# A product of constants in every slot of the quantised attention, and four query heads of batch two turned by transposes on TensorE

## What is computed

```
q = (x @ Wq + bq).reshape(1, B * N, H, hd)          # 256 queries, 16 heads of 16
kv = (cond @ Wkv + bkv).reshape(1, -1, 2, H, hd)    # 4096 keys and values
q, k, v = q * scale (hd ** -0.5), kv[:, :, 0], kv[:, :, 1]
q = _fq_sym(q, axis=-1)       # rounded to 127 steps of each row's largest
k = _fq_sym(k, axis=-1)
v = _fq_sym(v, axis=2)
attn = softmax(einsum('bhqd,bhkd->bhqk', q, k))
attn = _fq_unsigned(attn, axis=-1)                  # 255 steps of each row's largest
out = einsum('bhqk,bhkd->bhqd', attn, v) @ Wp + bp
```

## Time and profile before

| | us |
|---|---|
| median of the runs (3) | 698.59 |
| lowest and highest run | 698.45, 702.17 |
| profiled execution, its own time | 700.33 |
| its span, first to last instruction | 699.0 |
| PE busy in the span | 659.5 (94%) |
| DVE busy | 573.9 (82%) |
| ACT busy | 413.6 (59%) |
| POOL busy | 389.1 (56%) |
| mean granted TensorE clock | 0.873 |

### The profile page before, as it was taken

The page is one execution under the profiler, slowest core; times in us unless marked ns, Lnnn a source line. Parts: engine busy times, 40 slices in busy tenths (PEclk is TensorE's granted clock), DMA queues, the critical chain, the costliest instruction groups (busy, mean ns, idle before and its releaser), DMA issues. The chain is left out here.

```text
span 699.0 us, 13832 instructions
## 1 busy us (share of the span) xinstructions
PE 659.5 (94%) x5080; PEld 400.2 (57%) x5080; DVE 573.9 (82%) x1029; ACT 413.6 (59%) x689; POOL 389.1 (56%) x500
## 2 busy tenths in 40 slices
PE   9899999999999999999999999888899699989996
PEld 7456766666666767767676667634354234333462
DVE  5998978887897797899898687987888697999555
ACT  5744454445444555647546345378889597799831
POOL 5878557585576636789963444555546333345401
PEclk9999999999999999999999999976568555555589
DMA  9565899656658599989867876679999699799900
GB/s 309 150 151 129 166 188 182 136 138 143 143 129 157 130 197 230 160 203 178 192 140 164 167 168 147 140 138 225 216 175 177 114 198 177 128 180 168 168 1 8
DMA packets 351219, 112.06 MB, mean 160 GB/s; under 512 B 317096, under 2 KB 347824, under 8 KB 351152
## 3 DMA queue, kind: packets, MB, share of 16 engines
q1 hardware_dynamic: 351152, 111.17, 78.1%
HBM read 31.97 MB, written 0.26 MB: 46 GB/s over the span
## 5 line engine op out<-in xcount | busy, mean ns | idle before, releaser
L1061 PE MATMUL psum<-c_nat,eT 128*128 128x256 f16 x1536 | 187.9, 273 | 1.5 <-ACT u_sb L1235 1.2
L1895 DVE TENSOR_REDUCE tops<-psum 128x1 f32<-128x512 f32 x256 | 160.2, 681 | 23.0 <-PE psum L1846 22.2
L1888 ACT ACTIVATE cT<-psum,bias,q_scale 128x1024 f16<-128x1024 f32 x128 | 153.2, 1202 | 27.1 <-PE psum L1846 25.6
L1033 PE MATMUL psum<-cT,qk 128*128 128x512 f16 x744 | 165.6, 379 | 0.1
L1061 PEld LDWEIGHTS psum<-c_nat,eT 128*128 128x128 f16 x1536 | 147.2, 98 | 24.5 <-issue 2.3
L1846 PE MATMUL psum<-kT,v_space 32*128 32x512 f16 x512 | 111.6, 556 | 14.3 <-DVE tops L1895 5.9
L1033 PEld LDWEIGHTS psum<-cT,qk 128*128 128x128 f16 x744 | 72.6, 98 | 82.3 <-issue 1.2
L1273 DVE TENSOR_REDUCE neg_max<-psum 128x1 f32<-128x2048 f32 x32 | 73.2, 2287 | 24.2 <-PE psum L1033 23.9
L1261 DVE TENSOR_TENSOR e_lo<-e_all,e_hi 128x2048 f16<-128x2048 f32 x32 | 87.8, 2744 | 0.0
L1204 ACT ACTIVATE e_all<-psum,neg_max 128x2048 f32<-128x2048 f32 x32 | 63.1, 1970 | 15.4 <-DVE neg_max L1275 15.4
L1846 PEld LDWEIGHTS psum<-kT,v_space 32*128 32x128 f16 x512 | 24.0, 97 | 77.6 <-DVE tops L1895 31.7
(11 more groups left out here) (283 smaller groups left out, 984.4 us busy)
## 6 DMA issues: line engine op xcount, KB each, us to landing
wvo_h<-in_L_xattn_Wv SPq DMA_DIRECT2D x30, 128.0 KB, 2.5
wvo_h<-in_L_xattn_Wo SPq DMA_DIRECT2D x30, 128.0 KB, 2.3
wqk_h<-in_L_xattn_Wq SPq DMA_DIRECT2D x28, 128.0 KB, 2.4
wqk_h<-in_wkT SPq DMA_DIRECT2D x28, 128.0 KB, 2.7
mx_land<-in_mx_weights SPq DMA_DIRECT2D x8, 384.0 KB, 4.1
v_space<-in_ctx SPq DMA_DIRECT2D x4, 512.0 KB, 5.6
cT<-in_ctx SPq DMA_DIRECT2D x2, 1024.0 KB, 9.0
c_nat<-in_expert_wT SPq DMA_DIRECT2D x2, 1024.0 KB, 6.7
```

Of the source, the lines that this page charges most:

```text
L1033: ins = pe.matmul(s_ps[:, n * 512:(n + 1) * 512], c.qk[:, u % 2, q_part, k, :], m.cT[:, b, c_part, 4 * n:4 * n + 4, k, :], start=(k, q_par ...
L1061: ins = pe.matmul(u_ps, c.eT[:, v % 2, e_part, j, :], m.c_nat[:, v // H0, c_part, j, :], start=(j, e_part, c_part) == (0, 0, 0), stop=(j, ...
L1888: act.activation(m.y[:, u % 2, q * CHUNK:(q + 1) * CHUNK], m.bank(second_place(u, q), 2), ACT.Exp, bias=m.bias[:, u:u + 1], scale=m.q_scal ...
L1895: dve.tensor_reduce(m.tops[:, n // NB, n % NB:n % NB + 1], m.bank(n % 3), AX.X, ALU.max, negate=True).then_inc(s["q_max"], 1)
```

## The change

It does two things.

The first: `pe_second` issues one `pe_idle_product` ahead of its two scores, into the first of the banks that these then fill, in every slot of units 1 to 31 (124 of them).

The second is in the turn of the queries. In each batch the first four heads (`NEAR`) are rounded by DVE at once into all eight places of a row (512 elements a partition), transposed by four fp16 transposes on PE into the side place and copied out by ACT (step `qT`, 512 elements). The other twelve are rounded once (192 elements), spread by POOL (1344 in place of 1536) and turned by the DMA as before, with 12 heads in place of 16. `pe_first` waits for ACT's copy at heads 0 of a batch, and for the DMA at head 4. Batch two's DMA turn stands behind unit 13's transposes (`QU_TURNED` 13, was 12). The step `both` is called `whole`, and the new step `qT` has a slot of its own: in slots, q 54, whole 55, qT 57 in batch two, so that the steps of output half 0 stand 1 or 2 slots later; everything from output half 1 (slot 69) on keeps its slot.

```diff
-QU_TURNED = 12
+QU_TURNED = 13
+NEAR = 4
...
-QU_WOVEN = "norm xT q both+spread"
+QU_WOVEN = "norm xT q whole qT+spread"
...
-QU_AT = dict(norm=(29, 1), apply=(29, 3), xT=(30, 1), q=(30, 3), both=(31, 0), spread=(31, 0))
+QU_AT = dict(norm=(29, 1), apply=(29, 3), xT=(30, 1), q=(30, 3), whole=(31, 0), qT=(31, 2), spread=(31, 0))
...
@@ pe_mix
-        pe.wait_ge(s["qu_turned"], 16 * b)
+        pe.wait_ge(s[f"qu_act{b - 1}"], QU_ACT["qT"])
...
@@ dve_queries
-    for part in range(2):
-        dve.tensor_scalar(m.q_rows[:, b, :, 0, part * HD1:(part + 1) * HD1], heads, ROUND, -ROUND, ALU.add,
-                          ALU.add).then_inc(sem, 1)
+    dve.tensor_scalar(m.q_rows[:, b, 0:NEAR], spread(heads[:, 0:NEAR], 2, P // HD1), ROUND, -ROUND, ALU.add,
+                      ALU.add).then_inc(sem, 1)
+    dve.tensor_scalar(m.q_rows[:, b, NEAR:, 0, :], heads[:, NEAR:], ROUND, -ROUND, ALU.add, ALU.add).then_inc(sem, 1)
...
@@ pe_queries
+    yield at["qT"]
+    pe.wait_ge(s[f"qu_dve{b}"], QU_DVE["near"])
+    for h in range(NEAR):
+        ins = pe.transpose(room[2].bitcast(FP16)[:, h * P:(h + 1) * P], flat(m.q_rows[:, b, h]), m.ident_fp16[:, :])
+    ins.then_inc(sem, 1)
+    yield from pe_leave(pe, room, at["qT"], s[f"qu_act{b}"], QU_ACT["qT"])
...
@@ act_queries
+    yield at["qT"]
+    act.wait_ge(s[f"qu_pe{b}"], QU_PE["qT"])
+    act.copy(flat(m.qT[:, b, 0:NEAR]), room[2].bitcast(FP16)[:, 0:NEAR * P]).then_inc(s[f"qu_act{b}"], 1)
...
@@ sp_queries
-    sp.dma_start_transpose(m.qT[:, b], flat(m.q_rows[:, b])).then_inc(s["qu_turned"], 16)
+    sp.dma_start_transpose(m.qT[:, b, NEAR:], flat(m.q_rows[:, b, NEAR:])).then_inc(s["qu_turned"], 16)
...
@@ pe_first
-    if n % (NB * H1) == 0:
-        pe.wait_ge(s["qu_turned"], 16 * (n // (NB * H1) + 1))
+    b, h = divmod(n // NB, H1)
+    if n % NB == 0 and h == 0:
+        pe.wait_ge(s[f"qu_act{b}"], QU_ACT["qT"])
+    if n % NB == 0 and h == NEAR:
+        pe.wait_ge(s["qu_turned"], 16 * (b + 1))
...
@@ pe_second
+    if u > 0:
+        pe_idle_product(pe, m, m.bank(second_place(u, q)))
     for k in range(CHUNK // BLK):
```

More of the change, by code:

```diff
@@ L111 @@
 EX_DVE = steps("logits best gap where where_f plus_one first second coef0 coef1 coef a0 a1 a2 a3 a4 a5 a6 a7 bias")
-QU_PE = steps("xT q")
-QU_ACT = steps("xT")
-QU_DVE = steps("biased amax clamp inverse over up both0 both1")
+QU_PE = steps("xT q qT")
+QU_ACT = steps("xT qT")
+QU_DVE = steps("biased amax clamp inverse over up near far")
 AT_PE = steps("yT0 out0 yT1 out1")
@@ L235, in __init__ @@
         self.qT = upper[:, 0:UNITS * P].rearrange("p (b h c) -> p b h c", b=B, c=P)
-        self.q_rows = upper[:, UNITS * P:2 * UNITS * P].rearrange("p (b h g r) -> p b h g r", b=B, h=H1, g=KG)
+        self.q_rows = upper[:, UNITS * P:2 * UNITS * P].rearrange("p (b h r d) -> p b h r d", b=B, h=H1, d=HD1)
         self.v_int = space[:, 0:KT * D // 2].bitcast(FP16).rearrange("p (t d) -> p t d", d=D)
@@ L1767, in dve_queries @@
     dve.reciprocal(qi, qs).then_inc(sem, 1)
-    yield at["both"]
+    yield at["whole"]
     dve.wait_ge(sem, QU_DVE["inverse"])
@@ L1797, in act_queries @@
     act_latents(act, m, b, room[0]).then_inc(sem, 1)
+    yield at["qT"]
+    act.wait_ge(s[f"qu_pe{b}"], QU_PE["qT"])
+    act.copy(flat(m.qT[:, b, 0:NEAR]), room[2].bitcast(FP16)[:, 0:NEAR * P]).then_inc(sem, 1)
 def pool_experts(pool, m, s, b, room, at, taken=None):
@@ L1815, in pool_queries @@
     yield at["spread"]
-    pool.wait_ge(s[f"qu_dve{b}"], QU_DVE["both1"])
-    pool.tensor_copy(m.q_rows[:, b, :, 1:KG, :], spread(m.q_rows[:, b, :, 0, :], 2, KG - 1)).then_inc(
+    pool.wait_ge(s[f"qu_dve{b}"], QU_DVE["far"])
+    pool.tensor_copy(m.q_rows[:, b, NEAR:, 1:, :], spread(m.q_rows[:, b, NEAR:, 0, :], 2, P // HD1 - 1)).then_inc(
         s["qu_pool"], 1)
@@ L2555, in perceiver @@
             queries = woven(QU_WOVEN, experts["add8"] + 1)
-            output = woven(OUT_WOVEN[0], queries["both"] + 1) | woven(OUT_WOVEN[1], NC * (H1 + 1) + 1)
+            output = woven(OUT_WOVEN[0], queries["qT"] + 1) | woven(OUT_WOVEN[1], NC * (H1 + 1) + 1)
             dilated = woven(DIL_WOVEN, output["added1"] + 1)
```

## The result

The changed kernel takes **704.07 us** (median of 20 runs, 701.35 to 709.4) beside 700.21 for the kernel before in the same session (20 runs). The ratio is 1.0058 with a 95% interval of 1.0043 to 1.0074: slower by 0.6%. The prediction said 682.3, with a range of 671 to 703, and 0.79 on faster. The median lies outside the range and on the other side. Over 20 runs the kernel before stands at 700.21, not at the 698.59 of its first three, so 1.6 us of the distance to 682.3 lie in the base that the forecast started from.

A forecast was written before the change was run, and what follows sets the result against it. At full clock the prediction took DVE or ACT, whichever has more to do, as the limit. 700.33 - 3.2 + 0.3 + 0.6 - 12.5 - 1.5 = 684.0, less 1.7: 682.3 us, range 671 to 703.

The forecast's parts named there:

- Base: Starting time: the profiled 700.33 us, less 1.7 us for the runs' median of 698.59.
- The turn of batch two: At unit 16, a PE wait of 1.1 us for ACT's copy replaces the 4.35 us DMA stall: -3.2 us.
- +0.3: In the queries' rounding, about 0.15 us more DVE work per batch, POOL off the path: +0.3 us.
- The turn of batch one: ACT's extra 0.57 us copy ahead of u_sb, which PE already waits for: +0.6 us, between 0 and 1.5.
- The clock: In the attention, products keep PE at 2.4 GHz; nine tenths of 13.9 us gained: -12.5 us.
- Rival B: In the attention, the clock rises sooner but falls again in thin stretches: 691 us, chance 0.20.
- The product itself: 124 products in the attention, 0.21 us each at 2.4 GHz, hidden by DVE at full clock: no cost.
- The limit of the gain: At full clock each attention stretch shrinks to the larger DVE or ACT time over 0.95: 13.9 us in all.
- rival D: In the attention, DMA transposes of the exponentials become the bound, +6 us: 689 us, chance 0.07.
- The last stretch: From 657.3 to 668.0 us, PE turns the last unit at the lower clock; full clock gives -1.5 us.
- C: In the attention, the clock doesn't answer to the product, whose PE time is paid: 715 us, chance 0.11.
- E: Only gaps in PE's work lower the clock; ending unit 16's stall restores it from there: 699 us, chance 0.05.

The follow-up runs named there:

- turn_only: The changed kernel without the product of constants, first four query heads still turned on PE in both batches: 698.44 us.
- product_only: The kernel before plus one product in each slot of units 1 to 31, all queries turned by DMA as before: 705.69 us.
- narrow: The changed kernel with its product on 32 rows instead of 128, same 512 columns: 715.06 us.
- two_products: The changed kernel with two products in each slot instead of one: 694.31 us.
- mix: The changed kernel with batch one's turn left to the DMA and two products a slot, but one in slots whose side work fills PE: 691.95 us.
- turn2_two: The changed kernel with two products in every slot and batch one's turn left to the DMA: 692.91 us.
- mix_less: As mix, but one product of 512 and one of 256 columns in the slots where mix has two: 696.38 us.

## Why the prediction was wrong, point by point

**Base.** The 1.7 us taken off for the runs' median came from three runs; 20 runs give 700.21, 0.1 under the profiled execution.

**The turn of batch two (-3.2): right on the spot.** The two slots across it took 3.9 us where they had taken 8.4, and the copy is waited for 0.43 where I had 1.1. The DMA turn hides, as said. Not foreseen is that part of it is given back in the neighbourhood: in turn_only slots 60 to 70 take 13.6 us for 12.9 and slots 50 to 58 14.2 for 13.7. The whole turn is worth -1.8 in the runs, where my three terms (-3.2, +0.3, +0.6) sum to -2.3.

**The turn of batch one (+0.6): right in size in the trace, not resolved by the runs.** The runs without a product say 0.96 with overlapping intervals, those with two 1.4, those with one -0.8. Both mechanisms that I named are in the trace: PE waits 0.69 us for DVE's rounding ahead of its transposes, and 0.66 for the u_sb behind ACT's copy. That is less than the 1.16 of the earlier trace rows, as PE itself comes later by then. PE's products behind u_sb start 1.22 us later than there (440.01 for 438.79); 0.58 of it is the copy, and 0.64 was there already when ACT began the exponentials ahead of it (434.92 for 434.28).

```profile
436.01 0.40 PE L1795 MATMUL psum<-ident_fp,v_space 128*128 128x128 f16 x4 [0.69 <-DVE v_space L1776]
...
438.82 0.58 ACT L1807 COPY v_space<-psum 128x512 f16<-128x512 f16 x1
439.39 0.47 ACT L1236 ACTIVATE u_sb<-psum,inv_sum 128x256 f32<-128x256 f32 x1
...
440.01 1.25 PE L1062 MATMUL psum<-c_nat,eT 128*128 128x256 f16 x10 [0.66 <-ACT u_sb L1236]
```

**The clock (-12.5): this is the step that failed.** Clock, product and last stretch were to give 14.0 us (12.5 and 1.5). The product alone, in product_only, costs 5.4 us, and 5.6 on top of turn_only (704.07 less 698.44). Of the 21.8 us between 682.3 and 704.07 that is 19.6; the base has 1.6 and the turn 0.5. I wrote "Some stretches will be low still (the start, behind the query wait), so I take nine tenths". One product a slot holds the full level for 0.40 of the stage (0.50 in product_only). I had reasoned that full-height work brings the level up (right: narrow doesn't, the product does) and took for granted that 124 of them are enough of it. Nothing in the trace of before said how many are: it had stretches with none and stretches with expert products in nearly every slot, and the thin slot with one product lay between. Two_products shows that the amount was the question: 0.92 with two. Rival B was the right mechanism, levels that alternate, at 0.20.

**The product itself (priced at nothing, "hidden by DVE"): right in thin slots at full clock, wrong elsewhere.** In the full stretch 564.1 to 570.9 DVE and ACT are busy without a gap, so the product costs nothing there. Where side work is thick it isn't hidden even at full clock: slots 39 to 50 have a clock of 1.00 in turn_only and in the changed kernel, and span 16.71 us without a product and 17.66 with it, 0.09 a slot. At 1.2 GHz it costs 0.14 a slot, 0.31 in a thin slot with value products (1.51 for 1.20), and without the clock's answer 16.6 us in all (narrow).

Rival B had "some 1.35 against DVE's 1.24: 0.1 over some 30 slots, +3". The price was nearly right. The sum of PE's time was sound: product, scores and a whole group of value products are 0.43 + 0.61 + 0.50 = 1.54 there, for 1.51 in the trace. Slots 117 to 120 came to 1.42 in the mean, and the same four take 1.31 in turn_only (645.84 to 651.06), so 0.11 more. What was wrong is the number of slots: the level is low in six tenths of the stage, not in 30 slots. With 0.6 x 16.6 = 10 in place of 3, rival B's 691 becomes 698. Of the 6 us still missing the base is 1.6, and the turn 1.4 (-1.8 in the runs for the -3.2 that B counts). The rest, some 3 us, lies in the 7 that B gave to the clock; no run splits it further.

**The limit of the gain: right in some stretches, wrong in others.** I took each stretch down to the larger of DVE and ACT over 0.95. Two_products and mix come near the full clock that this assumes, with more products inside (248 and 219 for 124). The stretches between the starts of the same exponentials, in us, each from one profiled execution:

| slots | before | forecast at full clock | turn_only | changed | two_products | mix |
|---|---|---|---|---|---|---|
| 4 to 15 | 19.2 | 16.2 | 19.3 | 18.8 | 17.2 | 17.0 |
| 15 to 25 | 13.0 | 13.0 | 13.0 | 13.6 | 14.9 | 13.6 |
| 25 to 39 | 24.6 | 21.2 | 25.3 | 26.2 | 24.9 | 24.6 |
| 39 to 50 | 16.9 | 16.9 | 16.7 | 17.7 | 19.1 | 18.1 |
| 50 to 58 | 13.7 | 12.7 | 14.2 | 14.6 | 14.2 | 13.2 |
| 60 to 70 | 12.9 | 12.9 | 13.6 | 14.7 | 13.6 | 14.6 |
| 70 to 100 | 50.9 | 46.9 | 51.2 | 51.6 | 47.8 | 46.4 |
| 100 to 123 | 35.6 | 33.1 | 35.6 | 37.9 | 35.4 | 34.7 |
| sum | 186.8 | 172.9 | 189.0 | 195.0 | 187.1 | 182.1 |

Of the 13.9 us there are 4.7 in mix and none in two_products. Slots 70 to 100 went as I said, 4 to 15 and 50 to 58 nearly. Slots 25 to 39 stay at 24.6, though DVE is busy only 20.19 of it, and the three stretches that I left unchanged grow by 3.5 us in mix; one of them, slots 39 to 50, grows at full clock with a single product too. Neither DVE (164.84 of 188.90) nor ACT (166.48) is within 5% of mix's stage. The prediction's own sign is met by both runs, with times of 694.31 and 691.95: "If the clock is full and the time above 690, the reading that DVE and ACT are the next limit within 5% failed".

How much of this is the price of the further products, no run shows. At the third product's 0.084 us the 95 that mix has more than the changed kernel would cost 8 us, an estimate; the 172.9 would then nearly be met by a kernel that held the level with one.

In slots 25 to 39 of two_products, at 1.00 all through, PE's longest waits are for the turned exponentials:

```profile
PE psum L1927 <- DMA c_nat<-cT: 2.0, 3, 1.1
```

They are 2.0 us in 3 waits. So chains between engines take part in that stretch, and rival D's wait for the DMA stands there, at 2.0 us in place of 6.

**The last stretch (-1.5): the size was right, the reason not.** From the start of the last exponential to the end it is 34.2 us for 36.0, though the level is full there only from 669.9 on, 1.3 us behind that start. Turn_only, where the level comes up some 4 us behind it, almost as late as before (5 us), has 34.7. So 1.3 of the 1.8 came without the product; why isn't shown.

**Where the 3.8 us of the profiled execution come from.** The stage starts 1.6 later (463.71 for 462.12), takes 3.6 more (202.5 for 198.9), in which the turn's 4.5 are gained and some 8 lost in the eight stretches of the table (turn_only, without a product, loses 2 of that, so that 6 are the product's); 0.4 is lost in the last slot, and the end is 1.8 shorter: +1.6 + 3.6 + 0.4 - 1.8 = +3.8.

**The rivals.** B happened, with a product at about its price there (0.11 to 0.14 for 0.1) but in more slots. C didn't happen in this kernel but in narrow. E, only gaps count, is shown wrong: from 632.4 on the level stayed down for 30.7 us in which PE was busy 30.70, and at 570.9 it fell behind 6.80 us with no wait of PE over 0.16. The Trainium skill's page "TensorE: Matmul & The Clock Gate", section "HAM oscillation — how this bites in real kernels", puts the loss of the clock down to idle gaps ("no PE-idle gaps"); here the clock is low with no idle at all, and in narrow it doesn't move with PE busier than in any other run (204.75 of 212.80). The same page of the Trainium skill, section "Part 3: Packing small matmuls — row/col tiling", says that matmuls on few rows leave most of the array idle, and narrow, whose product fills 32 rows and leaves the clock where it was, fits that.

## What to carry to other kernels

A filler that is to raise the clock may hold it, or hold it in part. Where it doesn't, its columns are paid at the lower clock, and the level swings (0.14 us a product here, though the product is 0.43 us of PE). Where it does, a product takes PE half as long and hides better, but not wholly (0.08 to 0.09 us on the path here where side work is thick or products are many). So a half-measure can be slower than none and than double: try one, two and three before you judge, and read the clock row beside the time to see in which case you are.

Price a filler in the state in which it would fail, that is at the lower clock, and against the time that the same slots take without it (here 27.9 us for 18 slots, 30.4 with it). A forecast that multiplies a gain by "nine tenths" for a state that no stretch of the trace shows should have its main weight on the row that is nearest to it.

## What the runs showed of the hardware

- In the changed kernel, one 128-row product of 512 columns a slot among matmuls that are mostly 32 rows high, the granted clock stays at 1.2 GHz for 30.70 us with PE busy 30.70. With two in every slot the full share of the stage is 0.92 and 0.96 (two_products, turn2_two), with one in 29 heavy slots and two elsewhere 0.98 (mix), with one and a half in place of the two 0.74 (mix_less).
- The same 512 columns on 32 rows don't move the clock (narrow, full share 0.14; none at all 0.14 to 0.16).
- A second product a slot, some 0.215 us of PE at full clock, makes the kernel 9.8 us faster, since the rest of PE's work is then through sooner (PE busy 175.51 us of the stage for 189.53); a third makes it 10.4 us slower.
- At the lower level the 32-row weight load behind a full-height product starts 0.52 us behind it (650.97 and 651.49), after 0.44 idle that ends in "issue". The group's 53.2 us of such idle are now the main wait of L1856's loads, but not a price by themselves: two_products has 57.9 and is faster, narrow has 2.2 and is no quicker in the slots where both are low.
